# Last attention of a four-layer network: one unit in four of the probabilities turned by a transposing DMA instead of TensorE

## The chip, the core and the metric

The kernel runs on one core of a Trainium2 chip. The metric is the device time of one execution in microseconds (us); lower is better. Inside the core, TensorE (PE) multiplies matrices, with a separate row for its weight loads (PEld). VectorE (DVE), ScalarE (ACT) and GpSimd (POOL) work on elements, and SyncE (SP) issues the DMAs. Each engine runs its own instructions in their order and waits on semaphores that others raise.

## The reference, cut to what matters

The network has four layers, each a cross-attention and a feed-forward part. Only the cross-attention of the last layer is touched. It has 2048 query rows (16 tiles of 128), 2048 keys, 16 heads of 16 columns, and rounds queries, keys, values and probabilities to integer steps:

```
q = _fq_sym(q, axis=-1); k = _fq_sym(k, axis=-1); v = _fq_sym(v, axis=2)
attn = jnp.einsum('bhqd,bhkd->bhqk', q, k)
attn = jax.nn.softmax(attn.astype(jnp.float32), axis=-1)
attn = _fq_unsigned(attn, axis=-1)      # s = max/255; clip(round(x/s), 0, 255) * s
out = jnp.einsum('bhqk,bhkd->bhqd', attn, v)
```

The rounded probability is a count from 0 to 255 times a step of its row. The largest probability of a row is always the count 255, so the count is `exp(score - max) * 255`, rounded. The kernel lets the exponential write it as a 16-bit integer.

## The kernel before

The program is a list of phases, one after the other. The phase concerned is `attend3`; it follows `qkv3`, which leaves turned keys `KT`, values `V` and turned queries, and it is followed by `moe`, which reads its result `attended` from memory.

The work is cut into units. A unit is one tile of 128 query rows, one head and one half of the keys (1024 keys). There are `UN` = 32 units in a tile of queries (two for each head, an even and an odd one), and `NU` = 512 in all. A unit passes through these steps:

- `score(u)` on TensorE: two matmuls of 512 keys write 1024 scores for 128 rows to one of three slots in PSUM (`S[:, u % 3]`, two banks each). From unit 3 on it waits for `exped` of unit u - 3, which had the slot.
- `maximum(u)` on VectorE: one reduction of 1024 scores for an even unit, two of 512 for an odd one, each as soon as its bank is there. `bias(u)` follows once for the two units of a head: a small reduction and a small multiply-add.
- `exp(u)` on ScalarE: writes the counts of the unit, 128 x 1024 16-bit integers, to one of four buffers (`ex[:, u % 4]`), and adds up the row.
- `turn(u)` on TensorE: eight transposes of 128 x 128 into one PSUM bank (`TPW`). There is one such bank, so it waits until the unit before it was evacuated.
- `evacuate(u)`: the bank is copied to one of four buffers (`pw[:, u % 4]`), for even units by ScalarE, for odd units by VectorE.
- `attend(u)` on TensorE: eight matmuls of the turned counts with the values, added up in one bank.

The order of each engine is written out. TensorE runs, for each u, `score(u)`, `turn(u - 4)`, `attend(u - 5)` (`LAG` is 4). ScalarE runs `exp(u)`, `evacuate(u - 2)`, `exp(u + 1)` for each even u. VectorE runs `maximum(u)`, `maximum(u + 1)`, `bias(u + 1)`, `evacuate(u - 3)` for each even u. After the last head of a tile there come `row_steps` (three small operations) behind the evacuation of the second unit pair, and `scale_rows` (between the two maxima of the third pair) and `scale_columns`, which finish the tile's output. SyncE loads the turned queries two tiles ahead, stores the output of each tile, and at the start issues the load of the weights of the next phase (5704 KB, `start_next`).

In the terms used below: a pair is the two units of one head (3 small steps and 2 large ones on VectorE, two exponentials on ScalarE). A group is two pairs, four units. There are 256 pairs and 128 groups.

Of the kernel before, what the change touches and what calls it, by code (L numbers as in the profile page):

```python
# [7 lines left out]
F16 = mybir.dt.float16  # L8
# [9 lines left out]
B = 16  # L18
# [2270 lines left out]
def attend3(nc, k, qT_in, steps, out, KT, V, v_step, load_next):  # L2289


    W3 = 3 * 32
    UK = B * P // 2
    UC = UK // P
    UN = 2 * NH
    NU = B * UN
    LAG = 4
    LN255 = 5.541263545158426
    with ExitStack() as ctx:
        def sb(name, shape, dt=F32):  # L2300
# [2 lines left out]
        s = semaphores(nc, ctx, "attend3_", """  # L2303
            weights_next q_loaded0 q_loaded1 o_stored0 o_stored1
            even_scores odd_scores unit_max row_max bias exped turned evacuated
            attended both row_recip probs_step scaled o_done""")
        S = k["psum"][:, 0:6, :].rearrange("p (u b) c -> p u (b c)", b=2)
        TPW = k["psum"][:, 6, :]
        TP = TPW.bitcast(BF16).rearrange("p (c m) -> p c m", m=P)
# [9 lines left out]
        pT = [pw[:, r].bitcast(F16).rearrange("p (c m) -> p c m", m=P) for r in range(4)]  # L2319
        block = ctx.enter_context(nc.Block())  # L2320

        @block.sync
        def _(sp):
            def load(t):
                if t >= 2:
                    sp.wait_ge(s["exped"], (t - 1) * UN)
                sp.dma_start(qt[:, t % 2], qT_in[t]).then_inc(s[f"q_loaded{t % 2}"], 16)

            def store(t):
                sp.wait_ge(s["o_done"], t + 1)  # L2330
                sp.dma_start(out[t], o[:, t % 2]).then_inc(s[f"o_stored{t % 2}"], 16)

            start_next, finish_next = load_next
            load(0)
            load(1)
            start_next(sp, s["weights_next"])
            for t in range(B):
                if t + 2 < B:
                    load(t + 2)
                store(t)  # L2340
            for j in range(2):
                sp.wait_ge(s[f"o_stored{j}"], B // 2 * 16)
            finish_next(sp, s["weights_next"])

        @block.scalar
        def _(act):
            def exp(u):
                t, h = u // UN, u % UN // 2
                if u % 2 == 0:
                    act.wait_ge(s["bias"], u // 2 + 1)  # L2350
                if u >= 4:
                    act.wait_ge(s["turned"], u - 3)
                nc.scalar.activation(ex[:, u % 4], S[:, u % 3], ACT.Exp, bias=mx[:, t % 2, h, 4:5], scale=steps[:, 0, t, h:h + 1],  # L2353
                                     accum_out=sums[:, t % 2, u % 2, h:h + 1]).then_inc(s["exped"], 1)

            def evacuate(u):
                act.wait_ge(s["turned"], u + 1)
                nc.scalar.copy(pw[:, u % 4], TPW).then_inc(s["evacuated"], 1)  # L2358

            for u in range(0, NU, 2):  # L2360
                exp(u)
                if u >= 2:
                    evacuate(u - 2)
                exp(u + 1)
            evacuate(NU - 2)

        @block.vector
        def _(dve):
            def maximum(u):
                t, h = u // UN, u % UN // 2  # L2370
                if u % 2 == 0:
                    dve.wait_ge(s["even_scores"], u // 2 + 1)
                    nc.vector.tensor_reduce(mx[:, t % 2, h, 0:1], S[:, u % 3], X, ALU.max).then_inc(s["unit_max"], 1)  # L2373
                else:
                    for b in range(2):
                        dve.wait_ge(s["odd_scores"], u - u % 2 + b + 1)
                        nc.vector.tensor_reduce(mx[:, t % 2, h, 1 + b:2 + b], S[:, u % 3, b * 512:(b + 1) * 512], X, ALU.max).then_inc(s["unit_max"], 1)  # L2377

            def bias(u):
                t, h = u // UN, u % UN // 2  # L2380
                dve.wait_ge(s["unit_max"], u // 2 * 3 + 3)
                nc.vector.tensor_reduce(mx[:, t % 2, h, 3:4], mx[:, t % 2, h, 0:3], X, ALU.max).then_inc(s["row_max"], 1)
                dve.wait_ge(s["row_max"], u // 2 + 1)
                nc.vector.tensor_scalar(mx[:, t % 2, h, 4:5], mx[:, t % 2, h, 3:4], steps[:, 1, t, h:h + 1], LN255, ALU.mult, ALU.add).then_inc(s["bias"], 1)  # L2384

            def evacuate(u):
                dve.wait_ge(s["turned"], u + 1)
                nc.vector.tensor_copy(pw[:, u % 4], TPW).then_inc(s["evacuated"], 1)  # L2388

            def row_steps(t):  # L2390
                j = t % 2
                dve.wait_ge(s["exped"], (t + 1) * UN)
                nc.vector.tensor_tensor(tot[:, j, 0], sums[:, j, 0], sums[:, j, 1], ALU.add).then_inc(s["both"], 1)
                dve.wait_ge(s["both"], t + 1)
                nc.vector.reciprocal(tot[:, j, 1], tot[:, j, 0]).then_inc(s["row_recip"], 1)
                dve.wait_ge(s["row_recip"], t + 1)
                nc.vector.tensor_scalar(tot[:, j, 2], tot[:, j, 1], 1e-8, COUNT_UNIT, ALU.max, ALU.mult).then_inc(s["probs_step"], 1)

            def scale_rows(t):
                j = t % 2  # L2400
                dve.wait_ge(s["probs_step"], t + 1)
                dve.wait_ge(s["attended"], (t + 1) * UN)
                if t >= 2:
                    dve.wait_ge(s[f"o_stored{j}"], t // 2 * 16)
                nc.vector.tensor_tensor(o[:, j].rearrange("p (h d) -> p h d", d=HD), O.rearrange("p (h d) -> p h d", d=HD),
                                        tot[:, j, 2].unsqueeze(2).to_broadcast([P, NH, HD]), ALU.mult).then_inc(s["scaled"], 1)

            def scale_columns(t):
                dve.wait_ge(s["scaled"], t + 1)
                nc.vector.tensor_tensor(o[:, t % 2], o[:, t % 2], v_step[:], ALU.mult).then_inc(s["o_done"], 1)  # L2410

            for u in range(0, NU, 2):
                t, at = u // UN, u % UN
                maximum(u)
                if t and at == LAG:
                    scale_rows(t - 1)
                maximum(u + 1)
                bias(u + 1)
                if u >= 4:
                    evacuate(u - 3)  # L2420
                if t and at == 2:
                    row_steps(t - 1)
                if t and at == LAG:
                    scale_columns(t - 1)
            evacuate(NU - 3)
            row_steps(B - 1)
            evacuate(NU - 1)
            scale_rows(B - 1)
            scale_columns(B - 1)

        @block.tensor
        def _(pe):
            def score(u):
                t, h = u // UN, u % UN // 2
                if u % UN == 0:
                    pe.wait_ge(s[f"q_loaded{t % 2}"], (t // 2 + 1) * 16)
                if u >= 3:
                    pe.wait_ge(s["exped"], u - 2)
                for b in range(2):
                    c = (u % 2) * UC + 4 * b  # L2440
                    last = nc.tensor.matmul(S[:, u % 3, b * 512:(b + 1) * 512], qt[:, t % 2, h * P:(h + 1) * P],  # L2441
                                            KT[:, c:c + 4, h // 2], start=True, stop=True)
                    if u % 2:
                        last.then_inc(s["odd_scores"], 1)
                if u % 2 == 0:
                    last.then_inc(s["even_scores"], 1)

            def turn(u):
                pe.wait_ge(s["exped"], u + 1)
                if u >= 1:  # L2450
                    pe.wait_ge(s["evacuated"], u)
                for c in range(UC):
                    last = nc.tensor.transpose(TP[:, c], counts[u % 4][:, c * P:(c + 1) * P], k["ident_b"][:])  # L2453
                last.then_inc(s["turned"], 1)

            def attend(u):
                t, h = u // UN, u % UN // 2
                pe.wait_ge(s["evacuated"], u + 1)
                if t and u % UN == 0:
                    pe.wait_ge(s["scaled"], t)  # L2460
                for c in range(UC):
                    kc = (u % 2) * UC + c
                    last = nc.tensor.matmul(O[:, h * HD:(h + 1) * HD], pT[u % 4][:, c], V[:, kc, h * HD:(h + 1) * HD],  # L2463
                                            start=kc == 0, stop=kc == B - 1)
                last.then_inc(s["attended"], 1)

            for u in range(NU + LAG + 1):
                if u < NU:
                    score(u)
                if LAG <= u < NU + LAG:  # L2470
                    turn(u - LAG)
                if u > LAG:
                    attend(u - LAG - 1)
# [622 lines left out]
```

## Time and profile before

| | |
|---|---|
| device time, median of 3 runs | 3113.32 us (3108.88 to 3116.57) |
| profiled execution: its own time | 3104.27 us |
| profiled execution: span of the trace | 3102.4 us |
| busy in the span: TensorE, VectorE, ScalarE, GpSimd | 80%, 68%, 53%, 17% |
| granted TensorE clock over the span | 0.928 of full speed |

The span is the time from the first to the last recorded instruction. Busy shares are averages over phases that are limited in different ways, so for a change in one phase the rows of that phase count. A bracket at the end of a row of the timeline is the idle time of the engine before the row, and what released it. A DMA is listed on the queue that issues it (SPq), with the time that the issue took; its landing time is given in the list of issues. The granted clock is a share of full speed: 1.00 is 2.4 GHz and 0.50 is 1.2 GHz.

### The profile page before, as it was taken

What the parts mean: (1) busy time and instruction counts of PE and PEld (TensorE: products, weight loads), DVE (VectorE), ACT (ScalarE), POOL (GpSimd) and SP (SyncE); (2) the same over time, 40 slices, a digit from 0 to 9 for tenths busy, and PEclk for the clock granted to TensorE, in tenths of its full rate; (3) what the DMA queues carried; (4) which work ended last, traced back from release to release, by engine and by line L of the source; (5) the groups of instructions that cost most, each with busy time, mean ns of one, the idle gap of its engine ahead of it and who ended that gap; (6) DMA issues with size and microseconds to landing.
All of it is one profiled execution on the core that took longest, in us unless ns stands there. A gap on an engine that the chain in (4) does not pass through costs nothing. (4 is left out here: it accounts for less than half of the span.)

```text
span 3102.4 us, 51049 instructions
## 1 busy us (share of the span) xinstructions
PE 2480.9 (80%) x19824; PEld 1684.5 (54%) x19848; DVE 2111.4 (68%) x4570; ACT 1629.7 (53%) x2787; POOL 529.9 (17%) x390
## 2 busy tenths in 40 slices
PE   7978999987999454587896667777777777779999
PEld 5755666764666232466565534444444444446666
DVE  6758778764332656575675779999999999942331
ACT  3434555442232444343442468888888888832322
POOL 2114343321221222321221400000000000011211
PEclk9999999998999666899998889999999999989999
DMA  3120000002000210211002220000000000010000
GB/s 132 32 79 7 11 8 11 6 4 82 21 21 11 88 31 7 72 36 44 22 18 85 72 97 15 8 8 15 8 8 15 8 10 14 3 33 11 21 11 11
DMA packets 59023, 92.84 MB, mean 30 GB/s; under 512 B 5521, under 2 KB 54689, under 8 KB 57761
## 3 DMA queue, kind: packets, MB, share of 16 engines
q1 hardware_dynamic: 58784, 89.57, 8.7%
q8 instruction: 161, 2.64, 0.4%
q14 instruction: 78, 0.63, 0.1%
HBM read 66.48 MB, written 23.07 MB: 29 GB/s over the span
## 5 line engine op out<-in xcount | busy, mean ns | idle before, releaser
L2353 ACT ACTIVATE attend_ex<-psum,attend_mx,queries_step 128x1024 uint16<-128x1024 f32 x512 | 618.4, 1208 | 125.4 <-DVE attend_mx L2384 125.4
L2453 PEld LDWEIGHTS psum<-ident_b,attend_ex 128*128 128x128 bf16 x4096 | 249.1, 100 | 399.0 <-issue 397.9
L2453 PE MATMUL psum<-ident_b,attend_ex 128*128 128x128 bf16 x4096 | 325.0, 224 | 154.8 <-DVE attend_pw L2388 123.7
L2441 PE MATMUL psum<-keys_turned,attend_qt 96*128 96x512 bf16 x1024 | 322.2, 398 | 86.4 <-ACT attend_ex L2353 75.1
L1274 PE MATMUL psum<-arena,moe_tokT 128*128 128x512 f32 (+2 forms) x896 | 361.5, 548 | 0.0
L2377 DVE TENSOR_REDUCE attend_mx<-psum 128x1 f32<-128x512 f32 x512 | 329.3, 685 | 26.0 <-PE psum L2441 7.6
L2373 DVE TENSOR_REDUCE attend_mx<-psum 128x1 f32<-128x1024 f32 x256 | 310.8, 1214 | 14.3 <-PE psum L2441 14.1
L1189 DVE TENSOR_TENSOR moe_h<-moe_sg,psum 128x512 f32<-128x512 f32 (+1 forms) x112 | 69.9, 625 | 273.6 <-PE psum L1274 265.6
L1274 PEld LDWEIGHTS psum<-arena,moe_tokT 128*128 128x128 f32 x896 | 166.4, 192 | 136.0 <-issue 121.1
L1050 ACT ACTIVATE moe_sg<-psum 128x512 f32<-128x512 f32 (+1 forms) x112 | 61.4, 548 | 297.3 <-PE psum L1274 293.1
L2463 PE MATMUL psum<-values,attend_pw 128*128 128x16 f16 x4096 | 180.0, 170 | 1.4 <-DVE attend_pw L2388 0.6
L1296 PE MATMUL psum<-arena,moe_hT 128*128 128x256 f32 (+1 forms) x800 | 178.9, 380 | 2.7 <-ACT moe_hT L1062 1.6
L2388 DVE COPY attend_pw<-psum 128x512 f32<-128x512 f32 x256 | 174.2, 680 | 5.0 <-PE psum L2453 5.0
L994 POOL IOTA moe_index<- 128x8 f32 x2 | 0.3, 142 | 1014.7 <-POOLq L67 1014.7
L1296 PEld LDWEIGHTS psum<-arena,moe_hT 128*128 128x128 f32 (+1 forms) x800 | 150.8, 190 | 28.2 <-issue 3.3
L2463 PEld LDWEIGHTS psum<-values,attend_pw 128*128 128x128 f16 x4096 | 159.6, 97 | 3.6 <-issue 3.0
L2358 ACT COPY attend_pw<-psum 128x512 f32<-128x512 f32 x256 | 150.0, 586 | 21.4 <-PE psum L2453 7.9
L1014 POOL TENSOR_TENSOR moe_h<-moe_h,moe_cw 128x1408 f32<-128x1408 f32 (+1 forms) x32 | 90.6, 2832 | 378.1 <-DVE moe_h L1189 378.1
L2441 PEld LDWEIGHTS psum<-keys_turned,attend_qt 96*128 96x128 bf16 x1024 | 59.4, 98 | 111.2 <-ACT attend_ex L2353 93.0
L883 PE MATMUL psum<-arena,gqa_oT 128*128 128x256 f32 x512 | 113.1, 379 | 0.0
L831 PE MATMUL psum<-arena,gqa_hT 128*128 128x512 f32 x256 | 112.9, 594 | 0.0
L1060 ACT COPY moe_hT<-psum 128x512 f32<-128x512 f32 (+1 forms) x112 | 54.1, 527 | 110.6 <-PE psum L1286 110.6
(420 smaller groups left out, 4784.1 us busy)
## 6 DMA issues: line engine op xcount, KB each, us to landing
queries_turned<-qkv_qT SPq DMA_DIRECT2D x16, 384.0 KB, 3.1
attend_qt<-queries_turned SPq DMA_DIRECT2D x16, 384.0 KB, 3.3
arena<-in_moe SPq DMA_DIRECT2D x1, 5704.0 KB, 18.4
arena<-in_gqa SPq DMA_DIRECT2D x1, 5440.0 KB, 18.7
arena<-in_moe SPq DMA_DIRECT2D x1, 4360.0 KB, 13.7
xatt_ct<-in_ctx_T SPq DMA_DIRECT2D x32, 128.0 KB, 2.2
residual<-xatt_y SPq DMA_DIRECT2D x32, 128.0 KB, 2.0
moe_xt<-residual SPq DMA_DIRECT2D x16, 256.0 KB, 3.0
```

Source lines behind the costliest of these rows:

```text
L831: last = nc.tensor.matmul(BIG[:, b], hT[:, ic], wq[:, ic, b * 512:(b + 1) * 512], start=ic == 0, stop=ic == DC - 1)
L883: last = nc.tensor.matmul(Y, oT[:, c], wo[:, c], start=c == 0, stop=c == GH - 1)
L1274: last = nc.tensor.matmul(bank[:, q % 2, 0:size], tokT[:, i % 2, j, ic], wt[:, ic, at:at + size], start=ic == 0, stop=ic == DC - 1)
L1296: last = nc.tensor.matmul(YB[:, j * D:(j + 1) * D], hT[0:size, j, c], wd[0:size, c], start=c == 0, stop=c == DN - 1)
L2353: nc.scalar.activation(ex[:, u % 4], S[:, u % 3], ACT.Exp, bias=mx[:, t % 2, h, 4:5], scale=steps[:, 0, t, h:h + 1], accum_out=sums[:, t % ...
L2358: nc.scalar.copy(pw[:, u % 4], TPW).then_inc(s["evacuated"], 1)
L2373: nc.vector.tensor_reduce(mx[:, t % 2, h, 0:1], S[:, u % 3], X, ALU.max).then_inc(s["unit_max"], 1)
L2377: nc.vector.tensor_reduce(mx[:, t % 2, h, 1 + b:2 + b], S[:, u % 3, b * 512:(b + 1) * 512], X, ALU.max).then_inc(s["unit_max"], 1)
L2388: nc.vector.tensor_copy(pw[:, u % 4], TPW).then_inc(s["evacuated"], 1)
L2441: last = nc.tensor.matmul(S[:, u % 3, b * 512:(b + 1) * 512], qt[:, t % 2, h * P:(h + 1) * P], KT[:, c:c + 4, h // 2], start=True, stop=True)
L2453: last = nc.tensor.transpose(TP[:, c], counts[u % 4][:, c * P:(c + 1) * P], k["ident_b"][:])
L2463: last = nc.tensor.matmul(O[:, h * HD:(h + 1) * HD], pT[u % 4][:, c], V[:, kc, h * HD:(h + 1) * HD], start=kc == 0, stop=kc == B - 1)
```

## The change

Every fourth unit (u % 4 == 3, the odd unit of every second head) is turned by a transposing DMA that SyncE issues. It reads the counts from `ex[:, u % 4]` and writes the turned counts to `pw[:, u % 4]`, with no PSUM bank and no evacuation. The remaining units are turned and evacuated as they were: the even ones by ScalarE, those with u % 4 == 1 by VectorE. All counts on `turned` and `evacuated` go through `on_pe(u)`, which leaves every fourth unit out. `exp(u + 4)` waits for `landed` in place of `turned` where it takes the buffer of such a unit, and `attend(u)` waits for `landed` in place of `evacuated`. The load of the next weights is issued by ScalarE's queue at the start of the phase instead of SyncE's. The stores and query loads of SyncE are put between its transposes.

```diff
+        def on_pe(u):
+            return u + 1 - (u + 1) // 4
...
+            def turn(u):
+                sp.wait_ge(s["exped"], u + 1)
+                if u >= 4:
+                    sp.wait_ge(s["attended"], u - 3)
+                sp.dma_start_transpose(out=pT[u % 4], in_=ex[:, u % 4].bitcast(F16)).then_inc(s["landed"], 16)
...
-            start_next, finish_next = load_next
             load(0)
             load(1)
-            start_next(sp, s["weights_next"])
-            for t in range(B):
-                if t + 2 < B:
+            for u in range(3, NU, 4):
+                t, at = u // UN, u % UN
+                turn(u)
+                if at == UN - 1 and t + 2 < B:
                     load(t + 2)
-                store(t)
+                if t and at == 15:
+                    store(t - 1)
+            store(B - 1)
...
         def _(act):
-                if u >= 4:
-                    act.wait_ge(s["turned"], u - 3)
+                if u >= 4 and u % 4 < 3:
+                    act.wait_ge(s["turned"], on_pe(u - 4))
+                if u >= 4 and u % 4 == 3:
+                    act.wait_ge(s["landed"], u // 4 * 16)
...
             def evacuate(u):
-                act.wait_ge(s["turned"], u + 1)
+                act.wait_ge(s["turned"], on_pe(u))
...
+            load_next[0](act, s["weights_next"])
...
         def _(dve):
-                if u >= 4:
+                if u >= 4 and (u - 3) % 4 == 1:
                     evacuate(u - 3)
...
-            evacuate(NU - 1)
...
         def _(pe):
             def turn(u):
                 pe.wait_ge(s["exped"], u + 1)
                 if u >= 1:
-                    pe.wait_ge(s["evacuated"], u)
+                    pe.wait_ge(s["evacuated"], on_pe(u - 1))
...
             def attend(u):
-                pe.wait_ge(s["evacuated"], u + 1)
+                if u % 4 < 3:
+                    pe.wait_ge(s["evacuated"], on_pe(u))
+                else:
+                    pe.wait_ge(s["landed"], (u // 4 + 1) * 16)
...
-                if LAG <= u < NU + LAG:
+                if LAG <= u < NU + LAG and (u - LAG) % 4 < 3:
                     turn(u - LAG)
```

## Rows read from the trace of the kernel before

**Rows 1.** The page's first line.
```profile
span 3102.4 us, 51049 instructions
```

**Rows 2.** Busy time in two stretches: length, engines' us (instructions), granted clock, DMA.
```profile
900.00:1100.00 200.00, 142.06 (x597) 95.55 (x599) 81.06 (x255) 71.84 (x120) 34.08 (x24) 0.82 0.12 40
...
1800.00:2737.00 937.00, 702.42 (x9216) 431.26 (x9216) 883.64 (x1615) 788.39 (x1280) 0.00 (x0) 0.96 0.05 16
```

**Rows 3.** Groups of instructions by line, 2000 to 2700 us: busy us, mean ns, idle before.
```profile
L2353 ACT ACTIVATE attend_ex<-psum,attend_mx,queries_step 128x1024 uint16<-128x1024 f32 x387 | 467.4, 1208 | 89.5 <-DVE attend_mx L2384 89.5
L2377 DVE TENSOR_REDUCE attend_mx<-psum 128x1 f32<-128x512 f32 x388 | 249.6, 685 | 17.8 <-PE psum L2441 3.7
```

**Rows 4.** Timeline, one pair of all engines: start us, us, engine, line, operation.
```profile
2304.84 0.61 PE L2441 MATMUL psum<-keys_turned,attend_qt 96*128 96x512 bf16 x2 [0.32 <-ACT attend_ex L2353]
2304.94 0.21 DVE L2384 TENSOR_SCALAR attend_mx<-attend_mx,queries_step 128x1 f32<-128x1 f32 x1
2305.07 0.68 DVE L2388 COPY attend_pw<-psum 128x512 f32<-128x512 f32 x1
2305.18 1.21 ACT L2353 ACTIVATE attend_ex<-psum,attend_mx,queries_step 128x1024 uint16<-128x1024 f32 x1 [0.41 <-DVE attend_mx L2384]
2305.66 1.21 DVE L2373 TENSOR_REDUCE attend_mx<-psum 128x1 f32<-128x1024 f32 x1
2305.86 0.46 PEld L2453 LDWEIGHTS psum<-ident_b,attend_ex 128*128 128x128 bf16 x8 [0.92 <-issue]
...
2306.29 0.19 ACT L2353 ACTIVATION_READ_ACCUMULATOR attend_ex<-psum,attend_mx,queries_step 128x1 f32 x1
...
2306.54 0.59 ACT L2358 COPY attend_pw<-psum 128x512 f32<-128x512 f32 x1
2306.54 0.60 PE L2441 MATMUL psum<-keys_turned,attend_qt 96*128 96x512 bf16 x2
2306.96 1.29 DVE L2377 TENSOR_REDUCE attend_mx<-psum 128x1 f32<-128x512 f32 x2
```

**Rows 5.** Timeline, the end of a tile of queries.
```profile
2330.45 0.16 DVE L2393 TENSOR_TENSOR attend_tot<-attend_sums 128x16 f32<-128x16 f32 x1
...
2332.15 0.41 DVE L2405 TENSOR_TENSOR attend_o<-psum,attend_tot 128x256 f32<-128x256 f32 x1
...
2334.94 0.98 PE L2453 MATMUL psum<-ident_b,attend_ex 128*128 128x128 bf16 x8 [1.17 <-DVE attend_pw L2388]
```

**Rows 6.** Timeline of SyncE's queue: query loads, one for each tile of queries.
```profile
2037.07 0.31 SPq L2327 DMA_DIRECT2D attend_qt<-queries_turned  x1
...
2094.58 0.31 SPq L2327 DMA_DIRECT2D attend_qt<-queries_turned  x1
...
2268.07 0.31 SPq L2327 DMA_DIRECT2D attend_qt<-queries_turned  x1
...
2326.05 0.31 SPq L2327 DMA_DIRECT2D attend_qt<-queries_turned  x1
```

**Rows 7.** Busy time by stretch, behind the idle time of TensorE in rows 5.
```profile
2335.00:2338.00 3.00, 3.00 (x35) 2.40 (x36) 2.62 (x5) 2.31 (x5) 0.00 (x0) 0.50 0.14 49
```

**Rows 8.** Timeline, two pairs in a stretch at half the clock.
```profile
1932.67 1.21 ACT L2353 ACTIVATE attend_ex<-psum,attend_mx,queries_step 128x1024 uint16<-128x1024 f32 x1 [0.62 <-DVE attend_mx L2384]
...
1936.83 1.20 ACT L2353 ACTIVATE attend_ex<-psum,attend_mx,queries_step 128x1024 uint16<-128x1024 f32 x1 [0.62 <-DVE attend_mx L2384]
```

**Rows 9.** The page's DMA issues: count, KB each, median us from issue to landing.
```profile
attend_qt<-queries_turned SPq DMA_DIRECT2D x16, 384.0 KB, 3.3
arena<-in_moe SPq DMA_DIRECT2D x1, 5704.0 KB, 18.4
...
mbit_cr<-in_ctx SPq DMA_DIRECT2D x8, 256.0 KB, 4.1
...
attended<-attend_o SPq DMA_DIRECT2D x16, 128.0 KB, 1.7
```

**Rows 10.** The page's DMA queues: packets, MB, their time as a share of 16 engines' span.
```profile
q1 hardware_dynamic: 58784, 89.57, 8.7%
```

More of the change, by code:

```diff
@@ L2305, in attend3 @@
             even_scores odd_scores unit_max row_max bias exped turned evacuated
-            attended both row_recip probs_step scaled o_done""")
+            attended both row_recip probs_step scaled o_done landed""")
         S = k["psum"][:, 0:6, :].rearrange("p (u b) c -> p u (b c)", b=2)
@@ L2331, in store @@
                 sp.dma_start(out[t], o[:, t % 2]).then_inc(s[f"o_stored{t % 2}"], 16)
-            start_next, finish_next = load_next
             load(0)
             load(1)
-            start_next(sp, s["weights_next"])
-            for t in range(B):
-                if t + 2 < B:
+            for u in range(3, NU, 4):
+                t, at = u // UN, u % UN
+                turn(u)
+                if at == UN - 1 and t + 2 < B:
                     load(t + 2)
-                store(t)
+                if t and at == 15:
+                    store(t - 1)
+            store(B - 1)
             for j in range(2):
                 sp.wait_ge(s[f"o_stored{j}"], B // 2 * 16)
-            finish_next(sp, s["weights_next"])
+            load_next[1](sp, s["weights_next"])
         @block.scalar
@@ L2386, in evacuate @@
             def evacuate(u):
-                dve.wait_ge(s["turned"], u + 1)
+                dve.wait_ge(s["turned"], on_pe(u))
                 nc.vector.tensor_copy(pw[:, u % 4], TPW).then_inc(s["evacuated"], 1)
```

## The prediction

> **What bounds the kernel now.** I read the stretches first. The phase that is changed runs from 1800 to 2737 us, 937 us of a span of 3102.4; VectorE is busy in 883.6 us of it (94%), ScalarE in 788.4, TensorE in 702.4 at a mean clock of 0.96 [rows 1, 2]. That invites the reading that VectorE is the bound and that each of its copies is worth its 0.68 us. The idle times speak against it: inside 700 us VectorE still waits 17.8 us in front of the reductions of odd units, and ScalarE waits 89.5 us for the bias [rows 3]. The timeline of one pair decides.
>
> Follow one pair [rows 4]. The bias starts at 2304.94, and the exponential of the even unit at 2305.18, 0.24 later. Its accumulator read ends at 2306.48. TensorE starts the scores of the odd unit three units on, which take the same PSUM slot, at 2306.54, 1.36 after the exponential started. The first half of those scores lets the reduction start at 2306.96 (0.42 later). The two halves take 1.29 (to the next step 1.32), the small reduction 0.20, and the next bias begins. The sum is 0.24 + 1.36 + 0.42 + 1.32 + 0.20 = 3.54 us: one pair. No copy of VectorE lies in this loop. A second loop has the same length: bias to copy 0.13, copy to the transposes 0.79 (2305.86), transposes and attend to the scores 0.68 (2306.54), then again 0.42 + 1.32 + 0.20 = 3.54. VectorE's own work is 0.20 + 0.13 + 0.59 (copy, start to next start) + 1.12 (large reduction of 1.21, if the next followed as closely as it follows the copy) + 1.32 = 3.36, so it waits some 0.18 for the odd scores. So three limits stand at 3.54, 3.54 and 3.36 us, and only the second and the third contain what the change removes. A group of two pairs is 7.08 us.
>
> Eight groups would make a tile of queries 56.7 us. The loads of the queries, one in each tile, are 57.51 us apart at full clock (2037.07 to 2094.58) and 57.98 apart in most later tiles (2268.07 to 2326.05) [rows 6]. So the end of a tile costs 0.8 us, and 0.5 more where the clock falls. It falls behind the 1.17 us in which TensorE waits for a copy of VectorE that the tile's small operations made late [rows 5], and is 0.50 for about 3 us [rows 7].
>
> **The change, part by part.**
>
> *Steady state.* In each of 128 groups eight transposes (0.42 us of TensorE) and one VectorE copy (0.59) go. The even pair of a group loses neither. In the other pair the second loop is gone, the third falls to 2.77, but the first stays at 3.54: it is made of the exponential, the scores, the maxima and the bias, and nothing of these is touched. ScalarE keeps four exponentials and two copies: 4 x 1.36 + 2 x 0.59 = 6.62 of 7.08. So I cost the removal at nothing. The bound on the other side is that VectorE was the limit after all: 128 x 0.59 = 75 us gained.
>
> *The transfer.* Call L the time from the end of an exponential to the landing of its turned unit, with SyncE's wake-up and issue in it. TensorE comes to `attend` of that unit only behind the scores of five units on and one turn. The chain that decides is: landing, attend 0.27, scores of the next odd unit 0.42, maxima to the next exponential 1.32 + 0.44, one pair 3.54, then exponential 1.36, copy 0.59, exponential 1.36, next transfer but one. That is L + 9.3 us for two groups, so below L = 14.16 - 9.3 = 4.9 us it costs nothing. Above, a group takes (L + 9.3)/2. From L = 6.6 on another loop is longer: the exponential four units on writes the buffer that the transfer reads, so a group takes L + 1.36.
> What is L? The trace has no transposing DMA. The nearest transfers are the 128 KB store from the same kind of buffer (1.7 us), the 384 KB load (3.3) and the slowest of 256 KB (4.1, three such in one go) [rows 9]. A unit is 256 KB. I take 3.5 us and, with wake-up, at most 4.1: covered, by 0.8 us or more. The upper bound by rows: if it is cut into 256-byte pieces (a block of 128 columns), it is 1024 packets, and a packet took 0.087 x 16 x 3102 / 58784 = 73 ns [rows 10], so 1024 x 73 / 16 = 4.7 us on 16 engines, over the 1.7 of the store: 6.4 us. Both ends are kept: no cost, or the rival below.
> The Trainium skill ("Advanced Engine Details and Errata", X-Bar Transpose (TRN2)) says that transposing DMAs are as fast as regular ones; no run here shows that yet, and by it the sum would be as I take it.
>
> *SyncE.* Its queue gains 128 issues. Query loads follow the last transpose of a tile, stores the fourth; both have tens of microseconds of room (a tile is 57 us). The wait for `attended` of four units earlier ends in front of, or some 0.5 us behind, the wait for the exponential; this is within the allowance for L.
>
> *End of a tile.* The first small operations (0.56 us, `row_steps`) now come in a pair with no VectorE copy, and take the place of its 0.59: they cost nothing. `scale_rows` in front of the odd maximum still costs 0.33 less the 0.18 of slack, and its effect on `attend` a little more: 0.2 to 0.4 in place of 0.8. With 0.4 for 15 tiles that is 6 us gained. Bounds: 0 and 12 (all of the 0.8).
>
> *The clock.* Waits of TensorE change. The 1.17 shrinks to about 0.7, as its VectorE copy comes earlier by those 0.56; the low stretches behind it cost 0.5 us in some ten tiles, so up to 5 us come back. But each group has a new gap: where the turn is missing, the 0.32 in which TensorE waits for the even scores [rows 4] grows by 0.42 to about 0.74. I take 3 us gained; the bad end is a rival.
>
> *Start.* The weight load (18.4 us, 5704 KB [rows 9]) now starts beside the first query load instead of behind it and shares its 16 DMA engines; the first scores wait for that. I take 1.5 us, bounds 0 and 4. The first transfer of a turned unit, some 14 us in, shares with the weights too: 1 us, bounds 0 and 5. ScalarE's own issue (0.4 us) lies in front of an exponential that has not got its bias yet: nothing.
>
> *End.* The last unit no longer goes through turn (0.7 at the end), copy (0.7) and attend in a row, but through L. Even, within 1 us.
>
> *Sum.* 3104.3 (own time of the profiled execution) - 6 - 3 + 2.5 + 0 = 3097.8. That execution was 9.0 us below the median of the runs shown (3113.3); the expected median is 3097.8 + 9.0 = 3107, 0.2% below before.
>
> **The rivals.**
>
> *A. The transfer comes too late (slower).* L is over 4.9. At the 6.4 us of the bound a group takes 7.85 instead of 7.08: 128 x 0.77 = 99 us more, some 3206. TensorE would wait for the landing in each group, with longer gaps than 0.7, so the clock may fall as well. For it: 2-byte elements must be scattered over partitions, and only about a microsecond is spare. Against: 256 and 384 KB are moved in 4.1 us or less. Worse, the eight 128 x 128 blocks may be done one after another, each at the 1.7 us of the smallest store: L = 13.6, a group 15.0, 1010 us more.
> The Trainium skill ("VectorE: DVE Perf Modes", The three transpose paths) gives 1309 ns for one 128 x 128 block by DMA against 390 for TensorE. No row shows it; as an estimate eight such blocks in sequence are 10.5 us, a group 11.8, and the kernel 610 us slower. If most of it is a fixed part, it agrees with my 3.5 instead.
> Chance of A: 0.24, of it 0.06 for blocks in sequence.
>
> *B. TensorE loses its clock (slower).* At half clock a pair took 4.16 us (1932.67 to 1936.83) [rows 8] instead of 3.54. In a pair without a copy only the first loop remains, with scores 0.2 slower: about 3.8. A whole phase so would be 128 x (4.16 + 3.8 - 7.08) = 113 us slower, half of it 56. For it: TensorE's share falls from 75% to about 69%, and a stretch at 71% had a clock of 0.82 [rows 2]. Against: a pause of 0.92 between weight loads in each pair passes at full clock as it is [rows 4], and the fall shown comes behind 1.17. From a third of the phase at half clock on it decides: +38 us, 3145. Chance 0.16.
>
> *C. VectorE was the bound (faster).* The copies are worth 75 us: 3032. For it its 94%; against it the 17.8 us and the loop of 3.54 without a copy. Chance 0.04.
>
> **How the numbers follow.** About 0.3% (9 us) can be told from no change. My own case (0.56) spans 3092 to 3114 and is centred 6 us below before: a third of it faster, nearly all else the same. Faster: 0.04 + 0.19, and 0.02 for a tile end worth more, 0.25. Same: 0.35. Slower: 0.24 + 0.16 = 0.40. The range for 8 in 10 is 3090 to 3210: it takes in A at 6.4 us and most of B, and leaves out C and blocks in sequence. The likeliest case's own range is 3092 to 3114.
>
> **What would show it.** That the change does what it says: 256 ScalarE and 128 VectorE copies, 3072 transposes on TensorE, 128 transposing issues on SyncE. If I am right, the first exponentials of pairs stay 3.54 us apart in both pairs, VectorE idles some 0.7 us in every second pair in front of the odd maximum, and `attend` does not wait for a landing. Query loads would be 57.1 us apart. A period of 7.08 with L above 5, or a shorter pair at full clock, would make the loops wrong; a wait of TensorE or ScalarE for the landing makes A right; a clock under 0.9 with L short makes B right.

## The result, and the profile after

The changed kernel takes 3155.7 us (median of 4 runs, 3148.9 to 3157.2) against 3112.5 before (4 runs). The ratio of the means (all ratios below are of means, and each is to runs of the kernel before that were taken with it) is 1.0134, with a 95% interval of 1.0115 to 1.0154: 43 us slower. The forecast was 3107, no change that can be told, and it was wrong. The time lies inside the stated range of 3090 to 3210, but only because the range takes in the rivals, and it lies where rival B puts it.

The profiled execution took 3157.2 us, 53 more than that of before. The first rows are the page's span, the granted clock in 40 slices (tenths), and one stretch (length, busy us and instructions of PE, PEld, DVE, ACT, POOL, clock, DMA share, GB/s) of the changed kernel. They answer to [rows 1, 2].

```profile
span 3155.4 us, 49024 instructions
...
PEclk9999999998998666898998777767777677779999
```

```profile
1800.00:2790.00 990.00, 776.12 (x8192) 482.03 (x8192) 822.96 (x1488) 783.88 (x1281) 0.00 (x0) 0.72 0.23 50
```

The clock of the phase fell from 0.96 to 0.72, and TensorE is busy for 776 us instead of 702 with a ninth of its instructions gone (8192 for 9216): it does less work and does it slowly. To compare the same 900 us of all kernels, here is that stretch, before and after, one answer each.

```profile
1830.00:2730.00 900.00, 676.65 (x8953) 415.69 (x8952) 857.46 (x1568) 765.98 (x1244) 0.00 (x0) 0.97 0.03 10
```

```profile
1830.00:2730.00 900.00, 720.34 (x7649) 447.97 (x7645) 767.00 (x1388) 730.76 (x1196) 0.00 (x0) 0.73 0.22 44
```

The timeline of the changed kernel shows one group at full clock around the end of a tile (start us, us, engine, line, operation; brackets: idle before, releaser). It answers to [rows 4].

```profile
2301.18 0.21 ACT L2367 ACTIVATION_READ_ACCUMULATOR attend_ex<-psum,attend_mx,queries_step 128x1 f32 x1
2301.42 1.23 SPq L2337 DMA_TRANSPOSE attend_pw<-attend_ex  x1
...
2301.97 1.20 ACT L2367 ACTIVATE attend_ex<-psum,attend_mx,queries_step 128x1024 uint16<-128x1024 f32 x1 [0.57 <-DVE attend_mx L2399]
...
2305.16 0.60 PE L2455 MATMUL psum<-keys_turned,attend_qt 96*128 96x512 bf16 x2 [0.84 <-ACT attend_ex L2367]
...
2305.51 1.20 ACT L2367 ACTIVATE attend_ex<-psum,attend_mx,queries_step 128x1024 uint16<-128x1024 f32 x1 [0.41 <-DVE attend_mx L2399]
```

The first exponentials of two pairs are 3.54 us apart (2301.97 to 2305.51), as before; this pair has a copy of VectorE. TensorE idles 0.84 us in front of the scores where a turn is missing. No wait for a landing stands here, and none stands in the list of waits from 2000 to 2700 us; the only one of TensorE in the phase is 0.67 us in front of its last `attend`. The next pair without a copy at full clock takes 3.55 us:

```profile
2320.64 1.20 ACT L2367 ACTIVATE attend_ex<-psum,attend_mx,queries_step 128x1024 uint16<-128x1024 f32 x1 [0.40 <-DVE attend_mx L2399]
...
2324.19 1.21 ACT L2367 ACTIVATE attend_ex<-psum,attend_mx,queries_step 128x1024 uint16<-128x1024 f32 x1 [0.57 <-DVE attend_mx L2399]
```

At half clock the same rows are 4.16 us apart for the pair with a copy and 3.76 for the one without:

```profile
2309.18 1.20 ACT L2367 ACTIVATE attend_ex<-psum,attend_mx,queries_step 128x1024 uint16<-128x1024 f32 x1 [0.70 <-DVE attend_mx L2399]
...
2313.34 1.20 ACT L2367 ACTIVATE attend_ex<-psum,attend_mx,queries_step 128x1024 uint16<-128x1024 f32 x1 [0.62 <-DVE attend_mx L2399]
...
2317.10 1.20 ACT L2367 ACTIVATE attend_ex<-psum,attend_mx,queries_step 128x1024 uint16<-128x1024 f32 x1 [0.62 <-DVE attend_mx L2399]
```

The clock does not stay down; it goes up and down. From 1830 to 2730 us it is at half speed 61 times, for 3 to 17.5 us each and some 480 us in all; before it was 11 times and some 55 us. Three stretches of 2 us of the changed kernel, the clock third from the end (0.50, 0.57, 1.00):

```profile
2314.00:2316.00 2.00, 2.00 (x22) 1.40 (x20) 1.73 (x3) 1.93 (x4) 0.00 (x0) 0.50 0.00 0
2316.00:2318.00 2.00, 1.84 (x20) 0.96 (x18) 1.91 (x6) 1.38 (x3) 0.00 (x0) 0.57 0.14 28
2318.00:2320.00 2.00, 1.42 (x26) 0.83 (x23) 2.00 (x3) 1.94 (x4) 0.00 (x0) 1.00 0.56 107
```

The last rows are those of the transfer (count, median us from issue to landing), of the DMA queues (packets, MB, share of 16 engines, to [rows 10]; q10 carries the weights, which were on q1 before) and of the start of the phase.

```profile
attend_pw<-attend_ex SPq DMA_TRANSPOSE x128, 3.1
```

```profile
q1 hardware_dynamic: 193808, 117.30, 13.7%
q10 hardware_dynamic: 144, 5.84, 0.5%
```

```profile
1804.28 0.77 SPq L2331 DMA_DIRECT2D attend_qt<-queries_turned  x2
1804.28 0.39 ACTq L2987 DMA_DIRECT2D arena<-in_moe  x1
...
1816.86 2.74 PE L2455 MATMUL psum<-keys_turned,attend_qt 96*128 96x512 bf16 x6 [18.37 <-DMA attend_qt<-queries_turned]
```

**Where the 53 us are.** The first query load is issued at 1804.3 instead of 1798.0: 6.3 us, all ahead of the phase, in code that the change does not touch. This point lay between 1798 and 1808 in the profiled executions of all kernels below, so it is variation from one execution to another. From that issue to the first scores it is 12.6 us instead of 3.6: 9.0. From the first scores to the end of the last attend it is 971.7 instead of 935.2: 36.5. The remaining 1.2 us come after. The second and the third are the change's.

### The profile page after: what moved, and what is told of

The parts are those of the page before. It is cut to its first block and busy times, and to the rows that moved or that the text cites. A ratio compares the mean times of both kernels' runs of the same rounds, so it can differ in the third digit from the quotient of the medians.

```text
span 3155.4 us, 49024 instructions
## 1 busy us (share of the span) xinstructions
PE 2562.4 (81%) x18824; PEld 1738.1 (55%) x18824; DVE 2051.3 (65%) x4442; ACT 1624.3 (51%) x2787; POOL 529.6 (17%) x390
## 5 line engine op out<-in xcount | busy, mean ns | idle before, releaser
L2455 PE MATMUL psum<-keys_turned,attend_qt 96*128 96x512 bf16 x1024 | 417.3, 501 | 152.1 <-ACT attend_ex L2367 133.6
L2467 PEld LDWEIGHTS psum<-ident_b,attend_ex 128*128 128x128 bf16 x3072 | 273.7, 125 | 261.4 <-issue 244.5
L2480 PEld LDWEIGHTS psum<-values,attend_pw 128*128 128x128 f16 x4096 | 180.5, 105 | 71.4 <-ACT attend_pw L2372 67.2
L2480 PE MATMUL psum<-values,attend_pw 128*128 128x16 f16 x4096 | 193.5, 175 | 4.2 <-DMA attend_pw<-attend_ex 0.7
L641 POOL TENSOR_TENSOR gqa_nq<-gqa_nq,neg_half 128x20 f32<-128x20 f32 x16 | 88.2, 5512 | 136.9 <-DVE gqa_nq L754 136.9
## 6 DMA issues: line engine op xcount, KB each, us to landing
arena<-in_moe ACTq DMA_DIRECT2D x1, 5704.0 KB, 20.5
```

## The experiments

There are two theories for the 36.5 us. **Clock**: the missing transposes leave TensorE too little to do, its clock falls, and every step on the loop that TensorE has gets longer. **Transfer**: the transposing DMA, its 33.6 MB of traffic or SyncE's work slows the phase, and the low clock only goes along with it. A separate theory, **start**, says that the 9.0 us come from the weights being loaded beside the first queries.

### The weights back on SyncE

```
 load(0)
 load(1)
+load_next[0](sp, s["weights_next"])     # and not on ScalarE
```

> The changed kernel with one thing put back: the load of the next weights is issued by SyncE behind the two query loads, not by ScalarE beside them. Theory: the first scores come 12.6 us behind the first query load's issue with the change and 3.6 before, and the weight load of 5704 KB beside it is the cause. Then the wait goes back to about 3.6, 9 us are regained (3156 to 3147), and the mean clock of the phase stays near 0.72. Rival: the late start comes from something else ahead of the phase; then the wait stays near 12 us and the time near 3156.

Measured 3148.2 us, ratio to before 1.0110 (1.0081 to 1.0140). The first rows show the wait of TensorE (issue of the query load at 1802.24 in this run):

```profile
1805.83 2.74 PE L2455 MATMUL psum<-keys_turned,attend_qt 96*128 96x512 bf16 x6 [9.38 <-DMA attend_qt<-queries_turned]
```

```profile
1830.00:2730.00 900.00, 723.26 (x7617) 449.64 (x7615) 764.40 (x1383) 727.83 (x1190) 0.00 (x0) 0.72 0.22 44
```

The wait is 3.6 us again (3.5 to 5.7 in all kernels with the weights behind the queries), and the clock has not moved. The two query loads landed in 16.5 us (median) in the changed kernel, in 4.1 here and in 4.1 before. So the start theory holds by the traces. The median falls by 7.5 us, but the intervals of the two ratios overlap, so the times alone would not show it. This kernel is the base of the next ones.

### TensorE's lost work put back, with nothing else

```
+def fill():
+    for c in range(8):
+        nc.tensor.transpose(SPARE[:, c % 4], k["ident_b"][:], k["ident_b"][:])
 if LAG <= u < NU + LAG and (u - LAG) % 4 < 3:
     turn(u - LAG)
+elif LAG <= u < NU:
+    fill()
```

`SPARE` is the half of the last PSUM bank that the phase does not use.

> As the run with the weights put back, and in each iteration that has lost its turn TensorE makes eight transposes of the constant identity, 128 x 128, into an unused half of the last PSUM bank. Nobody waits for them and nothing is evacuated, so the only thing restored is TensorE's own activity. Theory (clock): the phase is slow because the missing transposes leave TensorE idle and its clock falls. Then the clock of the phase goes from 0.72 to 0.95 or more, a group takes 7.08 us again and the time is 3147 - 45 = 3102. Rival (transfer): the transposing DMA, its traffic and SyncE's work slow the phase. Then it stays at 3147 or a little above, with a clock that may rise.

Measured 3104.6 us (10 runs), ratio to before 0.9976 (0.9961 to 0.9991).

```profile
1830.00:2730.00 900.00, 653.97 (x9030) 443.49 (x9030) 797.58 (x1454) 758.62 (x1256) 0.00 (x0) 0.97 0.23 46
```

The DMA share is 0.23 as with the change, so the transfers are all there, and yet 43.6 us are gone against the kernel without the filling. The clock went from 0.72 to 0.97 with more TensorE instructions and less busy time (654 against 723 us). The clock theory passes, and the transfer theory fails. What TensorE computes in those slots is used by nobody.

### The opposite: the work taken out of the kernel before

```
-for c in range(UC):
+for c in range(UC if u % 4 < 3 else 1):
     last = nc.tensor.transpose(TP[:, c], counts[u % 4]...)
```

> The kernel before, with seven of the eight transposes left out in every fourth unit (u % 4 == 3); the copy, its waits and all else stay, and there is no transposing DMA. Seven eighths of those units' turned probabilities are therefore stale: part of the computation is left out. Theory (clock): the clock falls as with the change, to about 0.7, and since each pair keeps a copy it is slower than the change per pair: 50 to 100 us over before, 3160 to 3210, although it does less work. Rival (transfer): no DMA, so no loss; the time is that of before or a few us less, 3105 to 3113.

Measured 3214.8 us, ratio 1.0325 (1.0297 to 1.0353).

```profile
1830.00:2730.00 900.00, 760.02 (x7234) 451.12 (x7233) 778.93 (x1404) 685.12 (x1114) 0.00 (x0) 0.61 0.03 9
```

With no transposing DMA at all (share 0.03) and seven transposes fewer in each group, the kernel before is 100 us slower. It loses more than the change does: the clock is lower (0.61 against 0.73), and both pairs of a group still hold a copy of VectorE between TensorE's steps, so 160 of the 242 pairs that its timeline shows take 4.1 us or more, against 41 of 255 with the change. Its tiles are 64.85 us apart. Together with the run before this one, the cause of the 36.5 us is shown from both sides: TensorE's work taken away without a transfer makes the phase slow, and given back beside the transfer makes it fast.

### A plain transfer in place of the transposing one

```
-sp.dma_start_transpose(out=pT[u % 4], in_=ex[:, u % 4].bitcast(F16))
+sp.dma_start(pw[:, u % 4], ex[:, u % 4].bitcast(F32))
```

> As the run with the weights put back, with a plain DMA of the same 256 KB in place of the transposing one; the units concerned are then copied unturned, so that part of the computation is wrong in its order. Theory (clock): the kind of transfer does not matter as long as it lands in time; 3147 within 4 us, clock near 0.72, no wait for the landing. Rival (transfer): the transposing itself disturbs; the time falls to 3125 or less with the clock unchanged.

Measured 3144.9 us, ratio 1.0113 (1.0080 to 1.0146), against 1.0110 with the transposing transfer: no difference that can be told.

```profile
attend_pw<-attend_ex SPq DMA_DIRECT2D x121, 256.0 KB, 2.3
```

```profile
1830.00:2730.00 900.00, 724.01 (x7644) 450.39 (x7641) 767.29 (x1387) 730.03 (x1195) 0.00 (x0) 0.73 0.12 44
```

The plain copy of 256 KB lands in 2.3 us and the transposing one in 3.1; both are covered. So the transposing costs 0.8 us of landing time, and none of the kernel's time that these runs can tell. It does load the DMA engines more: their share is 0.22 with it and 0.12 with the plain copy, against 0.03 before, so about twice the engine time for the same bytes.

### Where the filling stands, and how much

The first kernel moves the eight transposes to the end of the iterations with u % 4 == 0 (except at the end of a tile); the pause of 0.84 us stays. The second keeps the place and makes four.

```
-elif LAG <= u < NU:
-    fill()
 if u > LAG:
     attend(u - LAG - 1)
+if u > LAG and u < NU and u % 4 == 0 and u % UN != LAG:
+    fill()
```

> The changed kernel with the weights put back and eight transposes of the identity for each group, but at another place: behind the attend of every fourth iteration (u % 4 == 0), in front of a wait of 0.46 us, and not in the slot that lost its turn, where TensorE idles 0.84 us. Theory 1 (the long pause): the 0.84 us pause is what costs the clock; it is still there, so the clock stays near 0.72 and the time near 3148. Theory 2 (TensorE's work as a whole): as much work as in the run filled in the slot, so clock 0.95 or more and 3105.

> As the run filled in the slot (weights put back), with four transposes of the identity instead of eight; the pause shrinks from 0.84 to about 0.6 us, no longer than the one for VectorE's copy that stays in each group. Theory 1 (the long pause): clock above 0.9 and 3105 to 3115. Theory 2 (work as a whole): half of the missing work is back, so a clock between, 0.8 to 0.9, and 3120 to 3130.

Measured 3126.6 us (ratio 1.0039, 1.0026 to 1.0052) and 3122.4 (1.0035, 1.0023 to 1.0046). The stretch of the one and of the other:

```profile
1830.00:2730.00 900.00, 682.44 (x8674) 438.14 (x8673) 779.76 (x1418) 739.88 (x1221) 0.00 (x0) 0.91 0.22 45
```

```profile
1830.00:2730.00 900.00, 676.56 (x8396) 449.18 (x8396) 790.67 (x1434) 749.74 (x1235) 0.00 (x0) 0.87 0.22 46
```

Theory 1 wanted 0.72 for the first and over 0.9 for the second and is wrong on both. Theory 2 wanted 0.95 for the first, which had 0.91, and 0.8 to 0.9 for the second, which had 0.87. It is nearer, but misses the first time by some 22 us. At the same place, more filling gives a higher clock (none 0.72, four 0.87, eight 0.97): the amount counts. The pause alone does not decide, for it still stands in the first kernel at full clock, for instance here:

```profile
2309.77 0.61 PE L2455 MATMUL psum<-keys_turned,attend_qt 96*128 96x512 bf16 x2 [0.84 <-ACT attend_ex L2368]
```

Whether the place counts for the clock is not shown. The first kernel leaves out the ends of tiles and so has 888 transposes of the identity where the one filled with eight in the slot has 1016, and its 0.91 against 0.97 may come from the amount as well. For the time the place does count. The first kernel has the higher clock of the two and is not faster, because at half clock its eight transposes stand in front of the scores on the loop, and a pair without a copy takes 4.62 us (2354.31 to 2358.93) where it took 3.76:

```profile
2354.31 1.20 ACT L2368 ACTIVATE attend_ex<-psum,attend_mx,queries_step 128x1024 uint16<-128x1024 f32 x1 [0.62 <-DVE attend_mx L2399]
...
2355.69 1.01 PE L2488 MATMUL psum<-ident_b 128*128 128x128 bf16 x8
...
2356.49 1.06 PE L2455 MATMUL psum<-keys_turned,attend_qt 96*128 96x512 bf16 x2
...
2358.93 1.20 ACT L2368 ACTIVATE attend_ex<-psum,attend_mx,queries_step 128x1024 uint16<-128x1024 f32 x1 [1.48 <-DVE attend_mx L2399]
```

Which property of a stretch decides its clock is left open.

### More filling

```
 elif LAG <= u < NU:
     fill()                       # 8, as above
+if u > LAG and u < NU and u % 4 == 0 and u % UN != LAG:
+    fill(6)
```

> As the run filled in the slot with eight transposes, with six more at the end of every fourth iteration (u % 4 == 0, not at the end of a tile). In the run without them the clock still fell to half some 14 times for about 3.3 us, and each fall costs some 0.6 us. If more work keeps the clock up: clock 1.00 from 1830 to 2730 us, 3104.6 - 8 = 3097, below both kernels. Rival: the six transposes stand in front of the scores of an odd unit, on the loop, and cost 0.1 us in each group: 3110 or more.

Measured 3100.8 us, ratio 0.9955 (0.9941 to 0.9970): the lowest time of the kernels here that compute everything, 12 us below before. Its interval overlaps that of the kernel with eight transposes only (0.9961 to 0.9991), so the six more are not shown to gain time, only clock.

```profile
1830.00:2730.00 900.00, 682.29 (x9718) 467.21 (x9714) 799.33 (x1456) 758.70 (x1256) 0.00 (x0) 0.99 0.23 47
```

```profile
2040.55 0.57 SPq L2331 DMA_DIRECT2D attend_qt<-queries_turned  x1
2097.95 0.57 SPq L2331 DMA_DIRECT2D attend_qt<-queries_turned  x1
```

The clock is 0.99, and at that clock the six transposes in front of the scores do not lengthen the loop. The tiles between 1926.66 and 2612.00 are 57.1 us apart in the mean (12 tiles), which is what the prediction gave for them; before they were 57.98 in most tiles [rows 6].

### VectorE's copies taken away, TensorE left alone

```
+w = UK // 2 if u < 4 else 1
-nc.vector.tensor_copy(pw[:, u % 4], TPW)
+nc.vector.tensor_copy(pw[:, u % 4, 0:w], TPW[:, 0:w])
```

> The kernel before with VectorE's copy of an odd unit cut from 512 columns to 1 (from unit 4 on); all transposes stay, no DMA. What is left out is the evacuation of the odd units, so their probabilities are stale. Theory (the loop exponential, scores, maxima, bias): a pair stays at 3.54 us at full clock although VectorE has 0.6 us less to do in every pair; only the end of a tile gets some 0.5 us shorter: 3115 - 8 = 3107, or more if the clock falls. Rival (VectorE is the bound): 256 x 0.59 = 150 us less, 2965, a pair at 2.95 to 3.2.

Measured 3092.2 us, ratio 0.9939 (0.9922 to 0.9956). One pair of this kernel, in its timeline, and its stretch:

```profile
2301.18 0.15 DVE L2389 COPY attend_pw<-psum 128x1 f32<-128x1 f32 x1
2301.30 1.20 ACT L2353 ACTIVATE attend_ex<-psum,attend_mx,queries_step 128x1024 uint16<-128x1024 f32 x1 [0.57 <-DVE attend_mx L2384]
...
2303.08 1.29 DVE L2377 TENSOR_REDUCE attend_mx<-psum 128x1 f32<-128x512 f32 x2 [0.43 <-PE psum L2442]
...
2304.84 1.20 ACT L2353 ACTIVATE attend_ex<-psum,attend_mx,queries_step 128x1024 uint16<-128x1024 f32 x1 [0.57 <-DVE attend_mx L2384]
```

```profile
1830.00:2730.00 900.00, 690.79 (x9024) 423.20 (x9025) 747.94 (x1577) 742.34 (x1250) 1.50 (x3) 0.99 0.04 11
```

A pair is 3.54 us (2301.30 to 2304.84) with the copies all but gone. VectorE, 95% busy in the stretch before and 83% here, waits 0.43 us in front of the odd maxima. So VectorE was not the bound, and rival C is out: of 150 us that its copies last, 20 come back. Tiles are 56.86 us apart in the steady stretch (2034.15 to 2091.01) instead of 57.51 or 57.98, some 17 us over 16 tiles, which is most of these 20.

### All odd units by DMA

```
-for u in range(3, NU, 4):
+for u in range(1, NU, 2):       # SyncE; two landing semaphores in turn
...
-if u >= 4 and (u - 3) % 4 == 1:
-    evacuate(u - 3)             # VectorE: no copy left
...
+elif LAG <= u < NU and u % UN != 5:
+    fill()
```

> All odd units (two in four) turned by the transposing DMA, with two landing semaphores in turn, eight transposes of the identity in each slot that lost its turn (not where the tile's output is scaled), and the weights issued by SyncE. VectorE has no copy left. Theory (the loop of exponential, scores, maxima and bias): a pair stays 3.54 us; a transfer lands some 3.2 us behind its exponential, against 4.9 that are free, and SyncE's 1.25 us of issue fit into a pair; a tile of queries takes 56.9 us, as in the run with the copies cut, so 3090 to 3097, a few us below the run with one unit in four and more filling (3100.8). Rival: two transfers in flight at once slow each other or SyncE's queue, and TensorE waits for the landings: above 3115.

Measured 3104.0 us (12 runs), ratio 0.9974 (0.9961 to 0.9987).

```profile
2304.31 1.20 ACT L2368 ACTIVATE attend_ex<-psum,attend_mx,queries_step 128x1024 uint16<-128x1024 f32 x1 [0.57 <-DVE attend_mx L2399]
...
2307.85 1.20 ACT L2368 ACTIVATE attend_ex<-psum,attend_mx,queries_step 128x1024 uint16<-128x1024 f32 x1 [0.57 <-DVE attend_mx L2399]
```

```profile
1830.00:2730.00 900.00, 651.83 (x8951) 470.77 (x8949) 739.59 (x1335) 748.86 (x1259) 0.00 (x0) 0.95 0.51 83
```

The pair is 3.54 us once more. Twice the transfers (DMA share 0.51) still land in 3.1 us (median), and in the steady state they cost nothing that shows in the pair. The kernel is no better than the one with one unit in four and eight transposes (0.9976). The expected 3090 to 3097 was missed by 7 us, and the forecast rival (3115 and more) too. Most of the miss stands at the start. Here the first transfers are issued while the weight load (19.8 us from its issue at 1808.3 to its landing) is still under way, and land in 6.2 us (median of the first four); ScalarE waits 4.57 us for one of them:

```profile
1829.08 1.21 ACT L2368 ACTIVATE attend_ex<-psum,attend_mx,queries_step 128x1024 uint16<-128x1024 f32 x1 [4.57 <-DMA attend_pw<-attend_ex]
```

That pair takes 8.99 us (1822.74 to 1831.73), some 5 more than its neighbours. So a part of the rival is true, once, beside a large load. The other 2 us of the miss are not explained by these rows.

## Why the prediction was wrong

**What bounds the kernel** was right. The loop of 3.54 us without a copy of VectorE in it stood in the changed kernel (3.54 or 3.55 in 36 of its 128 pairs without a copy, the ones at full clock), in the one with all odd units by DMA, and in the one with the copies cut. That the removal is worth nothing in the steady state at full clock follows from it.

**The transfer** was right in its choice. The exponential's sums are done at 2301.39, SyncE issues at 2301.42, and the median landing follows 3.1 us later. L is 3.1 to 3.2 us, against the 3.5 to 4.1 taken and the 4.9 that are free. The upper bound of 6.4 came from 73 ns a packet, the mean over all packets, most of them larger than 512 bytes; these took some 21. The sentence on the Trainium skill ("Advanced Engine Details and Errata", X-Bar Transpose (TRN2)), that transposing DMAs are as fast as regular ones, does not quite hold here: the transposing one took a third longer to land (3.1 against 2.3 us for the same 256 KB). The estimate of 10.5 us for eight blocks in sequence, worked out in the prediction from the Trainium skill ("VectorE: DVE Perf Modes", The three transpose paths), was three times too long.

**The end of a tile** was right: 57.1 us expected, 57.1 in the kernel whose clock was kept.

**The start** failed in its size: 1.5 us with bounds of 0 and 4 were given, and 9.0 were measured. The first scores started 12.6 us into a weight load that landed after 20.5. The 1 us for the first transfer came out as nothing in the changed kernel, where that transfer was issued at 1827.6 with the weights landed; the stall of 4.57 us in the kernel with all odd units by DMA shows what it is when they are not. The load of 18.4 us itself [rows 9] was the bound that I should have written down.

**The clock** is the step at which the forecast failed. It said that the new gap of about 0.74 us would be borne and that 3 us would be gained. The gap was 0.84, the clock fell to 0.73 in the mean, and the phase took 36.5 us more. The argument against rival B, that a pause of 0.92 us between weight loads in each pair passes at full clock, compared one pause with another and left out that a ninth of TensorE's instructions went at the same time. The run with half of the filling shows that the amount counts; the one with the filling elsewhere kept the 0.84 us and had a clock of 0.91. Rival B had the mechanism and the prices: 4.16 us for a pair with a copy and 3.8 for one without, measured 4.16 and 3.76. Its sum is somewhat high: with half clock for 53% of the stretch it gives 113 x 0.53 = 60 us, less the some 6 of the tile ends and the 5 that falls cost before, and 36.5 came. Only 41 of the 127 pairs with a copy took 4.1 us or more; that the clock often changes inside a pair may be the reason, and no run separates it. What was wrong was its chance of 0.16. The row on which it stood (71% busy at a clock of 0.82) [rows 2] was a warning and no rule: it is of another phase, and the kernel with all odd units by DMA had TensorE busy for 72% of the stretch at a clock of 0.95.

## What to carry to other kernels

Taking work off an engine whose clock depends on its load can make everything that waits for it slower. When TensorE stands on the loop that sets the period, price the loop at both levels of its clock before work leaves it, and give the lower level a real chance: busy shares alone did not tell the two apart here. A run that puts the lost work back with nothing else tells whether the clock is the cause. Put such work where TensorE waits longest: in front of a step of the loop it costs time whenever the clock is low. Before an instruction is removed from the engine with the highest busy share, add up the loop that sets the period; if the instruction is not in it, its whole duration is worth only what it does at the seams.

## What was not expected of the hardware

- Eight transposes of a constant 128 x 128 identity in each group of four units (7.08 us at full clock), whose result nobody reads, brought the granted clock from 0.72 to 0.97 and 43.6 us back.
- The clock of the changed kernel moves between its two levels (0.50 and 1.00, 1.2 and 2.4 GHz) inside a steady loop, in which no matmul of TensorE waits for more than 0.93 us from 1830 to 2730 us; it stays at half speed for 3 to 17.5 us at a time; the stretches from 2314 to 2320 us show one rise.
- A load of 5704 KB issued on ScalarE's queue at the same moment as one of 384 KB on SyncE's held up the small one: the two query loads landed in 16.5 us (median) instead of 4.1, and the first scores started 12.6 us behind the issue instead of 3.6.
- A transposing DMA of 128 x 1024 16-bit elements inside the core's own memory took 3.1 us from issue to landing and held SyncE's queue for 1.23 us; a plain one of the same size landed in 2.3. Its packets are small and quick: q1 and q10 together have 135,168 packets more than before, and their time is (0.142 x 3155.4 - 0.087 x 3102.4) x 16 us, some 21 ns for each, against a mean of 73 before. Beside a weight load of 5704 KB the first four landed in 6.2 us in the kernel with all odd units by DMA.
